# A mixture-of-experts feed-forward over the two chosen experts only, with rows scattered and gathered through memory

## The chip, the cores and the metric

One core of one Trainium2 chip runs the whole kernel: TensorE (PE, with its weight loads shown apart as PEld), VectorE (DVE), ScalarE (ACT), GpSimd (POOL), and SyncE (SP), whose queue here only issues DMAs. The metric is the device time of one execution in microseconds, the median of three runs.

## The reference

Sixty-four sequences of 68 tokens (36 image patches, 32 words), 192 features each, are embedded, pass one quantised attention layer, and then a feed-forward layer with one shared network and eight experts, of which each token uses the best two:

```python
h = h + _L0_attn_ref(_layernorm(h), ...)
h = h + _L0_ffn_ref(_layernorm(h), ...)

def _L0_ffn_ref(x, w_fc_sh, w_proj_sh, w1, w2, router_w, balance_bias):
    shared = _mlp(x, w_fc_sh, w_proj_sh)              # square(relu(x @ wfc)) @ wproj
    scores = jax.nn.sigmoid(xf @ router_w.T)
    _, idx = jax.lax.top_k(scores + balance_bias, 2)
    tw = jnp.take_along_axis(scores, idx, axis=-1)
    tw = tw / (tw.sum(-1, keepdims=True) + 1e-20)
    combine = (jax.nn.one_hot(idx, E) * tw[..., None]).sum(1)
    h = jnp.square(jax.nn.relu(jnp.einsum('nc,ech->neh', xf, w1)))
    y = jnp.einsum('neh,ehc->nec', h, w2)
    return shared + jnp.einsum('nec,ne->nc', y, combine).reshape(x.shape)
```

There are T = 4352 tokens, 34 blocks (TT) of 128, 17 pairs of blocks. All weights are 192 x 192.

## The kernel before

The program is written engine by engine, with semaphores by hand and barriers between stages. The helper `pipeline` (L58) runs stages with lags, unrolls the first steps and loops over the rest. The embedding stage ends in a barrier at 181 us, the attention stages run to 662 us. Their code hardly changes. `split_high` (L668) and `split_low` (L959) split the scaled expert weights in float16 high and low parts, in five chunks laid beside the image steps, and `store_split` (L452) stores them in `w_split` in memory. `load_rest` (L504) loads them and the residual rows `hf` back late in the attention.

**From the projection to the routing.** After `y_scalars` (L1282), ScalarE quantises pairs of blocks (`y_whole`, L794). VectorE adds them (`residual`, L1285) and takes statistics (`stats`, L1292). `deviation` (L1297) follows in two parts. Then, for each pair, VectorE's `normal` (L1306) makes `xf`, ScalarE copies it to float16 (`x2_high`, L803), and VectorE makes the low part (`x2_low`, L1313). TensorE turns the rows (L1606), ScalarE copies them to `XS` (`x2_out`, L808), and `route` (L1594) multiplies them by the router's weights. When all 17 pairs are through, ScalarE takes the sigmoid (L826) and VectorE compares all pairs of experts for all blocks at once (L1336 to L1350, with instructions of 2176 elements). It writes the weight of each expert, zero for six of the eight, as three bfloat16 parts in `C3` (L1352). TensorE turns them to `CT`. A barrier follows.

**The feed-forward.** All nine networks, experts and shared, stand side by side as one of U = 1728 hidden features, in 14 chunks (UC) of 128. `chunks` (L352) walks over 17 groups of 256 tokens and, in each, over the 14 chunks. A chunk goes through `up` (L1628, five matmuls of 256 columns for the float16 parts), `relu` (L836) on ScalarE, `weigh` (L1361) on VectorE, which multiplies by the token's weights that `weights` (L1641) spreads over the partitions by a matmul, `square` (L615) on GpSimd, `high` (L842) on ScalarE, `low` (L1374) on VectorE, and `down` (L1653, six matmuls of 192 columns into one accumulator). The buffers of a chunk are sevenfold (HB). So 17 x (14 x 11 + 8) = 2754 matmuls. `add_h` (L1380) adds the residual, and SyncE stores the group. All matmuls are recorded at L1394, all plain ScalarE copies at L631.

Buffers lie in four big regions (R0, R1, R2, M), which the profile names R or M.

Of the kernel before, what the change touches and what calls it, by code (L numbers as in the profile page):

```python
# [44 lines left out]
HB = 7  # L45
WEIGHED = E * C // P
W2M = UC - 1
# [33 lines left out]
def program(nc, x, x_txt, tok_W, tok_b, tok_pos, embed, W1, b1, W2, b2, w_qkv, b_qkv, w_proj, b_proj,  # L81
            w_fc_sh, w_proj_sh, w1, w2, router_w, balance_bias, ident_c, headmask_c, select_c, lower_c, out):
    ctx = ExitStack()
    with ctx:
# [33 lines left out]
        w_dram = nc.dram_tensor("w_split", [P, 4 * U + 2 * UC * C], F16, kind="Internal").ap()  # L118
# [161 lines left out]
        hf = R2[:, 6144:6144 + TT * C].rearrange("p (i c) -> p i c", i=TT)  # L280

        o16 = [R1[:, 8704 + 512 * k:8704 + 512 * (k + 1)].bitcast(F16).rearrange("p (h t) -> p h t", h=2) for k in range(2)]
        q16 = R2[:, 12672:12672 + 3 * C].bitcast(F16).rearrange("p (a i c) -> p a i c", a=3, i=2)
        xf = R2[:, 13248:13248 + 4 * C].rearrange("p (a i c) -> p a i c", a=2, i=2)
        rows2 = R2[:, 14016:14016 + 4 * C].bitcast(F16).rearrange("p (a i c) -> p a i c", a=2, i=2)
        CT = R1[0:32, 8704:8704 + T // 2].bitcast(BF16)

        hr = R1[:, 0:7 * 256].rearrange("p (a t) -> p a t", a=HB)
        hc = R1[:, 1792:1792 + 7 * 256].rearrange("p (a t) -> p a t", a=HB)
        hs = R1[:, 3584:3584 + 7 * 256].rearrange("p (a t) -> p a t", a=HB)  # L290
        hh = [R1[:, 5376 + 896 * k:5376 + 896 * (k + 1)].bitcast(F16).rearrange("p (a t) -> p a t", a=HB) for k in range(2)]
        ost = R1[:, 7168:7168 + 2 * 2 * C].rearrange("p (a i c) -> p a i c", a=2, i=2)
        sel_b = R1[0:32, 11008:11008 + UC * P // 2].bitcast(BF16)

        w1a = R0[:, 13824:13824 + 2 * U]
        w2a = R1[:, 8456:8456 + UC * C].rearrange("p (m c) -> p m c", m=UC)
        rw_rows = R1[0:E, 11144:11144 + C + C1]
        wst = R0[:, 9216:9216 + 2 * 1344].bitcast(F16).rearrange("p (a k x) -> p a k x", a=2, k=2)
        w2f = w2a.rearrange("p m c -> p (m c)")
        WCH = [(w1a[:, 1152 * k:1152 * (k + 1)], 0, 1152 * k, 2 * U) for k in range(3)]  # L300
        WCH += [(w2f[:, 1344 * k:1344 * (k + 1)], 4 * U, 1344 * k, UC * C) for k in range(2)]
        WCH_AT = [(0, 2), (0, 5), (1, 3), (2, 1), (2, 4)]
        wsplit = R2[:, 0:2 * U + UC * C].bitcast(F16)
        w1s = [R2[:, U * k:U * (k + 1)].bitcast(F16) for k in range(2)]
        w2s = [R2[:, 2 * U + 1344 * k:2 * U + 1344 * (k + 1)].bitcast(F16).rearrange("p (m c) -> p m c", m=UC) for k in range(2)]


        XS = R0[:, T + TT * C:T + TT * C + 3 * T // 2].bitcast(F16).rearrange("p (k t) -> p k t", k=3)
        mv2 = R2[:, 14848:14848 + 2 * TT].rearrange("p (i s) -> p i s", s=2)
        rs2 = R2[:, 14920:14920 + 3 * TT].rearrange("p (k i) -> p k i", k=3)  # L310
        bst2 = R2[:, 15330:15330 + 6 * TT].rearrange("p (i s) -> p i s", i=TT)
# [4 lines left out]
        scr = [R2[:, 15330 + 272 * k:15330 + 272 * (k + 1)].rearrange("p (i e) -> p i e", e=E) for k in range(4)]  # L316

        cmp_a = R0[:, T:T + TT * E * E].rearrange("p (i e f) -> p i e f", e=E, f=E)
        cmp_b = R0[:, T + TT * E * E:T + 2 * TT * E * E].rearrange("p (i e f) -> p i e f", e=E, f=E)
        lower = misc(E * E)  # L320
        sel_w = R0[0:32, 1280:1280 + UC * P]
        xs = R0[:, 0:768].bitcast(F16).rearrange("p (a k t) -> p a k t", a=2, k=3)
        cts = R0[0:32, 1024:1280].bitcast(BF16).rearrange("p (a t) -> p a t", a=2)
        C3 = misc(TT * 16, BF16).rearrange("p (i e) -> p i e", i=TT)
        ex2 = misc(4 * TT).rearrange("p (k i) -> p k i", k=4)
        bmask = misc(4)
        csum = misc(2 * TT).rearrange("p (k i) -> p k i", k=2)


        turns = []  # L330
# [18 lines left out]
        def chunk_rows(m):  # L349
            return P if m < W2M else C1  # L350
# [1363 lines left out]
```

## Time and profile before

| | us |
|---|---|
| median of three runs | 1084.67 (1079.42 to 1090.14) |
| the profiled execution | 1084.4 |
| its span | 1082.6 |
| mean granted clock of TensorE | 0.747 |
| feed-forward stage, in the span | 780.8 to 1079.5 |
| stage from y_scalars to the feed-forward | 694.9 to 780.8 |

Times in the profile are in microseconds from the start of the span unless marked ns. A digit of a slice line is tenths of a fortieth of the span (27.07 us). PEclk is the clock granted to TensorE, in tenths of 2.4 GHz; 0.50 is 1.2 GHz. "Idle before, releaser" tells what ended the engine's idle time ahead of a group.

### The profile page before, as it was taken

The numbers are of one execution on the slowest core, as the hardware profiler recorded it, in microseconds if no ns is written. First come the engines' busy times: TensorE is split into PE (matmuls) and PEld (weight loads), VectorE is DVE, ScalarE is ACT, GpSimd is POOL, SyncE is SP. The second block draws the span as 40 slices with busy tenths as digits, with TensorE's granted clock in tenths as the row PEclk, the third lists the DMA queues.
The fourth block names the chain that finished last, engine by engine and source line by source line (L and its number), as shares of the span: only waits on it lengthen the run. The fifth ranks groups of instructions, "written<-read, shape, count | busy, mean of one in ns | idle before, by whom it ended". The sixth has DMA issues, their size and how long they took to land.

```text
span 1082.6 us, 24294 instructions
## 1 busy us (share of the span) xinstructions
PE 765.0 (71%) x7852; PEld 589.9 (54%) x7852; DVE 806.9 (75%) x1866; ACT 531.8 (49%) x1101; POOL 365.0 (34%) x370
## 2 busy tenths in 40 slices
PE   3699895247724774378888861206399999999998
PEld 2698795146512442145555441105177777777776
DVE  3334551589996999699999979997577777777776
ACT  3123340124427514278888873338155555555554
POOL 2120000358832120132323221000076666666665
PEclk9999798567775555555555555555599999999999
DMA  7942622200002221122222226000000100000000
GB/s 191 250 139 72 175 81 76 84 23 1 0 0 60 74 74 30 38 36 41 39 45 41 43 20 241 9 0 2 16 16 17 32 19 26 23 22 23 22 30 15
DMA packets 114142, 58.11 MB, mean 54 GB/s; under 512 B 75656, under 2 KB 107568, under 8 KB 113968
## 3 DMA queue, kind: packets, MB, share of 16 engines
q1 hardware_dynamic: 112768, 51.24, 18.8%
q0 software_dynamic: 1328, 6.30, 2.0%
q8 instruction: 24, 0.39, 0.1%
q14 instruction: 22, 0.18, 0.1%
HBM read 29.61 MB, written 9.83 MB: 36 GB/s over the span
## 4 chain that ended last, share of the span: by engine, by line
PE 42%; DVE 24%; issue 14%; SPq 9%; DMA 4%; ACT 4%; POOL 3%; DVEq 1%; POOLq 0%; ACTq 0%
PE ps L1394 38%; DMA R<-h_rows 2%; DVE R L1185 2%; DVE M L1091 2%; DVE M L1092 2%; SPq L473 2%; ACT R L631 2%; DVE M L1215 2%; DVE R L1210 1%; PE ps L1468 1%; DVE R L1198 1%; SPq L501 1%; DVE R L1192 1%; SPq L433 1%; DVE R L1290 1%
## 5 line engine op out<-in xcount | busy, mean ns | idle before, releaser
L1394 PE MATMUL ps<-R 128*128 128x192 f16 (+8 forms) x3618 | 460.4, 280 | 32.0 <-DVE R L897 14.4
L1394 PEld LDWEIGHTS ps<-R 128*128 128x128 f16 (+4 forms) x3618 | 348.3, 114 | 120.4 <-issue 59.4
L623 POOL TENSOR_TENSOR R<-R 128x256 f32<-128x256 f32 x238 | 195.5, 828 | 188.3 <-DVE R L1371 186.7
L1371 DVE TENSOR_TENSOR R<-R,ps 64x256 f32<-64x256 f32 (+1 forms) x272 | 114.0, 419 | 62.3 <-ACT R L840 42.4
L1394 PE MATMUL ps<-M 32*128 32x68 bf16 (+2 forms) x1152 | 98.4, 244 | 84.3 <-DMA M<-R 65.9
L840 ACT ACTIVATE R<-ps 128x256 f32<-128x256 f32 x238 | 91.1, 383 | 136.0 <-PE ps L1394 129.0
L631 ACT ACTIVATE R<-ps 68x896 bf16<-68x896 bf16 (+7 forms) x140 | 94.4, 677 | 110.7 <-PE ps L1468 44.9
L1394 PEld LDWEIGHTS ps<-M 32*128 32x128 bf16 (+2 forms) x1152 | 63.1, 115 | 135.3 <-issue 61.1
L631 ACT ACTIVATE R<-R 128x256 f16<-128x256 f32 (+5 forms) x281 | 125.5, 448 | 23.0 <-POOL R L569 20.5
L634 ACT ACTIVATE R<-R,sc 64x512 f16<-64x512 f32 (+12 forms) x106 | 82.8, 838 | 94.0 <-POOL R L586 41.1
L1378 DVE TENSOR_TENSOR R<-R 128x256 f16<-128x256 f32 x238 | 113.0, 476 | 20.1 <-ACT R L631 18.1
L600 POOL TENSOR_TENSOR R<-R,M 128x884 f32<-128x884 f32 x32 | 53.2, 1662 | 146.9 <-ACT M L754 146.9
L1553 PE MATMUL ps<-ident_b,R 128*68 128x128 bf16 x416 | 55.1, 303 | 22.0 <-ACT R L631 20.0
L1394 PE MATMUL ps<-M,R 128*68 128x192 f16 (+2 forms) x430 | 45.0, 258 | 27.1 <-DVE R L1267 26.8
L567 POOL TENSOR_TENSOR R<-R 68x768 f32 (+1 forms) x16 | 23.5, 1467 | 113.3 <-DVEq L1016 108.2
L1480 PE MATMUL ps<-ident,R 68*128 68x68 f32 x64 | 14.3, 295 | 64.2 <-ACT R L631 54.6
L1394 PEld LDWEIGHTS ps<-M,R 128*68 128x68 f16 (+2 forms) x430 | 40.3, 131 | 31.5 <-issue 18.3
L1553 PEld LDWEIGHTS ps<-ident_b,R 128*68 128x68 bf16 x416 | 40.8, 163 | 29.5 <-ACT R L631 26.0
L1394 PE MATMUL ps<-R,M 68*32 68x4 bf16 (+2 forms) x1680 | 54.0, 215 | 2.9 <-DVE R L1030 1.4
L1480 PEld LDWEIGHTS ps<-ident,R 68*128 68x128 f32 x64 | 11.6, 189 | 68.2 <-issue 56.0
L1185 DVE SCALAR_TENSOR_TENSOR R<-ps,sc,M 128x544 f16<-128x544 f32 x64 | 42.6, 707 | 6.9 <-PE ps L1394 5.9
L1394 PEld LDWEIGHTS ps<-R,M 68*32 68x32 bf16 (+1 forms) x1680 | 40.1, 115 | 13.6 <-issue 5.6
(235 smaller groups left out, 1002.0 us busy)
## 6 DMA issues: line engine op xcount, KB each, us to landing
R<-in_x_dram SPq DMA_DIRECT2D x12, 576.0 KB, 8.0
M<-R SPq DMA_DIRECT2D x16, 260.0 KB, 2.3
M<-R SPq DMA_DIRECT2D x32, 130.0 KB, 2.0
R<-h_rows SPq DMA_DIRECT2D x4, 816.0 KB
R<-h_rows SPq DMA_DIRECT2D x1, 3264.0 KB, 14.1
R<-R SPq DMA_DIRECT2D x17, 192.0 KB, 2.5
out_dram<-R SPq DMA_DIRECT2D x17, 192.0 KB, 2.0
R<-w_split SPq DMA_DIRECT2D x1, 3072.0 KB, 20.8
```

Source lines behind the costliest of these rows:

```text
L567: pool.tensor_tensor(v, hb[:, b4, :], mv[:, b4, 0:1].to_broadcast([N, 4, C]), ALU.subtract).then_inc(sem("centred"), 1)
L600: pool.tensor_tensor(L[par], L[par], S[:, par, 1, :].unsqueeze(2).to_broadcast([P, SLOTS, N]), ALU.subtract).then_inc(sem("relative"), 1)
L623: pool.tensor_tensor(hs[0:rows, m % HB, :], hr[0:rows, m % HB, :], other, ALU.mult).then_inc(sem("squared"), 1)
L631: return act.activation(out_, in_, ACT.Copy)
L634: return act.activation(out_, in_, ACT.Identity, scale=scale, bias=bias)
L840: act.activation(hr[0:rows, m % HB, :], ps[0:rows, m % 2, 0:256], ACT.Relu, scale=H_UNIT).then_inc(sem("relu"), 1)
L1185: last = dve.scalar_tensor_tensor(D[:, s0:s0 + 2 * k, :].rearrange("p (a s) k -> p a s k", a=2), score_part(0, part), s1(A_NKK), m.unsquee ...
L1371: last = tt(hc[rows, m % HB, :], hr[rows, m % HB, :], ps[rows, 2 + e % 2, 0:256], ALU.mult)
L1378: tt(hh[1][0:rows, m % HB, :], hs[0:rows, m % HB, :], hh[0][0:rows, m % HB, :], ALU.subtract).then_inc(sem("low"), 1)
L1394: return pe.matmul(o, a, b, start=start, stop=stop, skip_group_check=True)
L1480: pe.transpose(ps[:, 0, k * N:(k + 1) * N], xn[:, par, k, 0:P], ident[0:N, 0:N])
L1553: last = pe.transpose(pPT[:, i, :], slots(Pb[par])[:, at, :], ident_b[:, :])
```

## The change

The shared network still runs over every token, in 17 units of 256 tokens. The experts run only over the rows that chose them. Each expert has a region of CAP = T + 256 rows in a tensor in memory, `x_by_expert`. GpSimd scatters each block's rows there, twice, by the slots of its two experts. The slots are counted on the chip, in three windows of 5, 7 and 5 pairs of blocks. At the end VectorE makes a table, on the chip, of 41 tiles of 256 rows (34 if all were full, and 7 for what is left over): for each its expert and its first row. The pads after each expert's rows are zeroed by DMAs. TensorE and SyncE read the table into registers (`value_load`). Outputs of the tiles go to `y_by_tile` in memory; GpSimd gathers for each block its two rows, and VectorE adds them with their weights to `hf`.

Sixty-eight scatters and 68 gathers are indirect DMAs, of 128 rows of 768 bytes each. Order of the units: 10 shared, 41 routed, 7 shared (58), each with a step on every engine. A step's `down` is three units behind its `up`. Routed tiles are counted ready for the first gathers after 17 tiles, for the second window's after 31, for the third's after 41. `hs`, `hr`, and the hidden PSUM banks are twofold, `hh` and `hl` fourfold.

The diff, cut to its core:

```diff
+TOP = 2
+WB = 2 * 2 * P + 2 * C
+TILE = 256
+ROUTED = TOP * T // TILE + E - 1
+WINDOWS = [(0, 5), (5, 12), (12, 17)]
+SHARED_FIRST = 10
+        SEQ = [("s", i) for i in range(SHARED_FIRST)] + [("r", t) for t in range(ROUTED)] + [("s", i) for i in range(SHARED_FIRST, PAIRN)]
+        LAG = 3
+        READY = [(TOP * P * w.stop + E * (TILE - 1)) // TILE for w in WBLK[:-1]] + [ROUTED]
+        COMBINE_AT = []
+        for i in range(PAIRN):
+            free = SHARED_FIRST + READY[window_of(i)] + LAG + 5
+            COMBINE_AT.append(max(free, COMBINE_AT[-1] + 1.5 if i else 0))
+        COMBINE_AT = [math.ceil(at) for at in COMBINE_AT]
...
+        WCH_AT = [(0, 2), (0, 5), (1, 3), (2, 1), (2, 4), (3, 2)]
+        WCH_DMAS = [4, 8, 4, 2, 2, 2]
...
 @block.sync
-            sp.dma_start(sel_w, select_c).then_inc(sem("ffn_c"), 16)
+            sp.wait_ge(sem("zeros"), 1)
+            for k in range(E - 1):
+                at = E * CAP + TILE * k
+                sp.dma_start(xg[at:at + TILE, :].rearrange("(a p) c -> p a c", p=P), ZT).then_inc(sem("x_zeroed"), 16)
             sp.wait_ge(sem("w_split"), 16)
-            barrier(sp, "sp")
+            sp.wait_ge(sem("table"), 1)
+            for e in range(E):
+                at = sp.value_load(pad_at[0:1, e:e + 1], min_val=0, max_val=(E - 1) * CAP + T)
+                sp.dma_start(xg[bass.ds(at, TILE), :].rearrange("(a p) c -> p a c", p=P), ZT).then_inc(sem("x_zeroed"), 16)
+            sp.wait_ge(sem("x_zeroed"), 16 * (2 * E - 1))
+            sp.wait_ge(sem("scattered"), 16 * TOP * TT)
+            def load_tile(t):
+                wait(sp, "tile_turned", t - 3)
+                at = sp.value_load(table[t:t + 1, 1:2], min_val=0, max_val=XROWS - TILE)
+                sp.dma_start(xr[:, t % 4], xg[bass.ds(at, TILE), :].rearrange("(a p) c -> p a c", p=P)).then_inc(sem(f"xr{t % 4}"), 16)
+            def store_tile(t):
+                sp.wait_ge(sem("y_out"), t + 1)
+                sp.dma_start(yg[TILE * t:TILE * (t + 1), :].rearrange("(a p) c -> p a c", p=P), yr[:, t % 4]).then_inc(sem(f"yr{t % 4}"), 16)
...
 @block.gpsimd
-            chunks([(square, 0)])(pool)
+            pool.memset(ZT, 0.0).then_inc(sem("zeros"), 1)
+            for w, (first, end) in enumerate(WINDOWS):
+                pool.wait_ge(sem("slots"), w + 1)
+                for n in range(2 * first, 2 * end):
+                    for k in range(TOP):
+                        pool.indirect_dma_start(xg, bass.IndirectOffsetOnAxis(ap=slot[:, n, k:k + 1], axis=0), rows2[:, n, :], None).then_inc(sem("scattered"), 16)
+            pool.wait_ge(sem("y_slots"), 1)
+            for i in range(PAIRN):
+                ready = READY[window_of(i)]
+                for a in range(4):
+                    pool.wait_ge(sem(f"yr{a}"), 16 * len(range(a, ready, 4)))
+                wait(pool, "combined", i - 3)
+                for j in range(2):
+                    for k in range(TOP):
+                        pool.indirect_dma_start(gb[:, i % 4, j, k, :], None, yg[0:TILE * ready, :],
+                                                bass.IndirectOffsetOnAxis(ap=y_slot[:, 2 * i + j, k:k + 1], axis=0)).then_inc(sem(f"gathered{i % 4}"), 16)
...
 @block.scalar
+            for i in range(8):
+                y_whole(i)
+            roots(0)
+            y_whole(8)
+            y_whole(9)
+            x2_window(0)
+            sigmoids(0)
...
+            for u in range(UNITS + LAG + 1):
+                t = u - SHARED_FIRST
+                if 1 <= u <= UNITS:
+                    high(u - 1)
+                if 0 <= t + 1 < ROUTED:
+                    x_tile(t + 1)
+                if 0 <= t - LAG - 1 < ROUTED:
+                    y_tile(t - LAG - 1)
+                if u < UNITS:
+                    relu(u)
...
 @block.vector
+            residuals(0, 5)
+            variances(0)
+            residuals(5, 7)
+            deviations(0)
+            normals(0)
+            residuals(7, 9)
+            choose(0)
+            residuals(9, 11)
+            place(0)
+            residuals(11, 12)
+            variances(1)
+            residuals(12, 13)
+            deviations(1)
+            normals(1)
+            residuals(13, 15)
+            choose(1)
+            residuals(15, 17)
+            place(1)
+            variances(2)
+            deviations(2)
+            normals(2)
+            choose(2)
+            place(2)
+            make_table()
+            y_rows()
+            def relu2(u):
+                dve.wait_ge(sem("relu"), u + 1)
+                wait(dve, "low", u - 1)
+                h = ps[:, u % 2, :].rearrange("p (m t) -> p m t", m=2)
+                dve.scalar_tensor_tensor(hs[:, u % 2], h, H_UNIT, hr[:, u % 2], ALU.mult, ALU.mult).then_inc(sem("relu2"), 1)
+            def low(u):
+                dve.wait_ge(sem("high"), u + 1)
+                wait(dve, "h_used", u - 3)
+                tt(hl[:, u % 4], hs[:, u % 2, 0], hh[:, u % 4, 0], ALU.subtract)
+                part = hh[C1:P, u % 4, 1]
+                tt(part, hs[C1:P, u % 2, 1], part, ALU.subtract).then_inc(sem("low"), 1)
...
+            for u in range(STEPS):
+                if 1 <= u <= UNITS:
+                    low(u - 1)
+                if u < UNITS:
+                    relu2(u)
+                if u >= LAG + 1 and u - LAG - 1 < UNITS and SEQ[u - LAG - 1][0] == "s":
+                    add_shared(u - LAG - 1)
+                for i in range(PAIRN):
+                    if COMBINE_AT[i] == u:
+                        combine(i)
...
 @block.tensor
+            def up(u):
+                kind, i = SEQ[u]
+                w = weights_at(u)
...
+                wait(pe, "relu2", u - 1)
+                for m in range(2):
+                    o = ps[:, u % 2, TILE * m:TILE * (m + 1)]
+                    mm(o, w(0, P * m, P), hi, True, False)
+                    mm(o, w(0, P * m, P), lo, False, False)
+                    mm(o, w(1, P * m, P), hi, False, False)
+                    mm(o, w(0, 2 * P + P * m, P), both, False, False)
+                    last = mm(o, w(1, 2 * P + P * m, P), both, False, True)
...
+            for u in range(UNITS + LAG):
+                t = u - SHARED_FIRST
+                if 0 <= t + 1 < ROUTED:
+                    turn_tile(t + 1)
+                if u < UNITS:
+                    load_expert(u)
+                    up(u)
+                if u >= LAG:
+                    down(u - LAG)
```

In words, what is cut out. `turn_tile` turns six blocks of 128 of the loaded tile. `x_tile` copies them (768 elements) out of PSUM to `xs`, `y_tile` copies the 384 output elements of a tile to `yr`. `load_expert` reads the expert's offset into a register, and `weights_at` adds the constant offset of each operand to it. `down` has two times five matmuls of 192 columns. `combine` has four products with sum of 192 elements, with one wait in their middle. `choose` finds the best two of eight by maxima, on 80 or 112 elements; `place` turns counts from two small matmul groups (`rank`) into slots; `make_table` has some 30 instructions on up to 48 elements; `y_rows` has 13 on up to 544. About 22 small VectorE instructions for a triangle of ones and the regions' first rows are added ahead of the first barrier. The weights in `w_split` are laid out by expert, with zero padding gone, 4.1 MB in place of 3.1.

## Rows read from the trace of the kernel before

**Rows 1.** The page: VectorE and the other engines over the span, and TensorE's granted clock.

```profile
PE 765.0 (71%) x7852; PEld 589.9 (54%) x7852; DVE 806.9 (75%) x1866; ACT 531.8 (49%) x1101; POOL 365.0 (34%) x370
...
PEclk9999798567775555555555555555599999999999
```

**Rows 2.** Stages: length, busy PE, PEld, DVE, ACT, POOL, clock, DMA share, GB/s.

```profile
784.00:788.00 4.00, 4.00 (x32) 2.90 (x31) 3.15 (x8) 2.38 (x7) 2.46 (x4) 0.88 0.00 0
...
800.00:1060.00 260.00, 260.00 (x2420) 204.69 (x2418) 196.54 (x463) 143.45 (x418) 171.59 (x209) 1.00 0.08 24
```

**Rows 3.** Groups by form in the feed-forward, 800 to 1060 us.

```profile
L1394 PE MATMUL ps<-R 128*128 128x256 f16 x970 | 137.7, 273 | 0.0
...
L840 ACT ACTIVATE R<-ps 128x256 f32<-128x256 f32 x194 | 74.3, 383 | 109.5 <-PE ps L1394 102.4 <-POOL R L623 7.1
...
L1385 DVE SCALAR_TENSOR_TENSOR R<-ps,sc,R 128x384 f32<-128x384 f32 x15 | 9.3, 618 | 0.5
```

**Rows 4.** Timeline of the routing stage, TensorE: start, length, instructions.

```profile
731.26 0.82 PE L1612 MATMUL ps<-ident_f,R 128*128 128x128 f16 x6 [0.74 <-DVE R L1317]
...
734.05 0.82 PE L1612 MATMUL ps<-ident_f,R 128*128 128x128 f16 x6 [0.48 <-DVE R L1317]
...
751.44 0.72 PE L1394 MATMUL ps<-M,R 128*128 128x8 f16 x20
```

**Rows 5.** Groups by form from 694 to 781 us, ScalarE's copies.

```profile
L631 ACT ACTIVATE R<-ps 128x768 f16<-128x768 f16 x17 | 13.8, 810 | 4.2 <-PE ps L1612 4.1
...
L631 ACT ACTIVATE R<-R 128x384 f16<-128x384 f32 x17 | 8.8, 516 | 2.2 <-DVE R L1310 2.2
```

**Rows 6.** Timeline of the end of the routing, ScalarE and VectorE.

```profile
750.35 0.42 DVE L1317 TENSOR_TENSOR R<-R 128x256 f16<-128x256 f32 x1
...
753.81 0.49 ACT L826 ACTIVATE R<-ps,sc 128x272 f32<-128x272 f32 x1
754.19 1.68 ACT L631 ACTIVATE R<-R 32x1792 bf16<-32x1792 f32 x1
754.33 0.44 DVE L1336 TENSOR_TENSOR R<-R,M 128x272 f32<-128x272 f32 x1 [3.56 <-ACT R L826]
```

**Rows 7.** Groups by form in the attention, 440 to 650 us, VectorE.

```profile
L1210 DVE SCALAR_TENSOR_TENSOR R<-ps,sc,R 128x512 f32<-128x512 f32 x32 | 23.8, 743 | 1.8 <-ACT ps L745 1.8
```

**Rows 8.** Timeline of the attention, SyncE's queue.

```profile
475.26 3.52 SPq L501 DMA_DIRECT2D M<-R  x4
```

**Rows 9.** The page, DMA issues: count, KB each, median us to landing.

```profile
out_dram<-R SPq DMA_DIRECT2D x17, 192.0 KB, 2.0
```

**Rows 10.** Line 98 (waits on a count), TensorE's queue: ns min/median/max, first and last start.

```profile
L98 PEldq FUSED_REGOPS  x65: 37/46/65, 47.6 to 1057.9; - x65
```

**Rows 11.** Timeline of the stage that begins at y_scalars.

```profile
694.87 2.53 ACT L634 ACTIVATE R<-R,sc 128x384 f16<-128x384 f32 x4 [9.99 <-DVEq L1282]
...
699.40 0.30 DVE L1288 TENSOR_SCALAR R<-R,sc 128x384 f16<-128x384 f16 x1
...
700.80 0.30 DVE L1288 TENSOR_SCALAR R<-R,sc 128x384 f16<-128x384 f16 x1
```

**Rows 12.** Timeline of small VectorE instructions in a chain.

```profile
432.63 0.16 DVE L1147 TENSOR_TENSOR sc<-sc 128x1 f32<-128x1 f32 x1
432.83 0.15 DVE L1148 TENSOR_SCALAR sc<-sc 128x1 f32<-128x1 f32 x1
```

**Rows 13.** Timeline behind the first barrier, SyncE's queue.

```profile
181.41 29.10 SPq L473 DMA_DIRECT2D R<-h_rows  x4
```

**Rows 14.** Timeline of GpSimd, two indirect DMAs in a row.

```profile
20.17 0.94 POOL L550 DMA_INDIRECT R<-in_L_txt_tok_embed_dram,R  x1 [9.06 <-PE ps L1419]
21.45 0.94 POOL L550 DMA_INDIRECT R<-in_L_txt_tok_embed_dram,R  x1 [0.34 <-issue]
```

**Rows 15.** Line 550, the sixteen indirect DMAs: ns min/median/max, first and last start.

```profile
L550 POOL DMA_INDIRECT R<-in_L_txt_tok_embed_dram,R x16: 944/945/1103, 8.8 to 87.6; - x16
```

**Rows 16.** Stages again, a stretch of the query, key and value products.

```profile
240.00:260.00 20.00, 15.36 (x108) 12.79 (x107) 17.67 (x27) 8.45 (x17) 16.62 (x12) 0.67 0.00 1
```

More of the change, by code:

```diff
@@ L286, in program @@
[L286 to L293, printed above, removed]
@@ L804, in x2_high @@
                 act.wait_ge(sem("xf"), i + 1)
[L805 to L806 removed]
+                copy(rows2[:, 2 * i:2 * i + 2, 0:C], xf[:, i % 2]).then_inc(sem("x2_high"), 1)
             def x2_out(i):
@@ L848, in _, with sigmoids, x2_window @@
-            chunks([(relu, 0), (high, 3)])(act)
+            def sigmoids(w):
+                t = WBLK[w]
+                act.wait_ge(sem("routed"), WINDOWS[w][1])
+                act.activation(scores[:, t, :], ps[:, 6, t.start * E:t.stop * E].rearrange("p (i e) -> p i e", e=E), ACT.Sigmoid, scale=s1(W_RU)).then_inc(sem("sigmoid"), 1)
+            def x2_window(w):
+                first, end = WINDOWS[w]
+                for i in range(first, end + 1):
+                    if i < end:
+                        x2_high(i)
+                    if i > first:
+                        x2_out(i - 1)
@@ new lines, in _, with x_tile @@
+            for i in range(8):
+                y_whole(i)
+            roots(0)
[3 more added lines that the diff above has]
+            sigmoids(0)
+            for i in range(10, 14):
+                y_whole(i)
+            roots(1)
+            y_whole(14)
+            y_whole(15)
+            x2_window(1)
+            sigmoids(1)
+            y_whole(16)
+            roots(2)
+            x2_window(2)
+            sigmoids(2)
+            def x_tile(t):
+                act.wait_ge(sem("tile_turned"), t + 1)
+                wait(act, "h_psum", SHARED_FIRST + t - 2)
+                copy(xs[:, t % 3], ps[:, 4 + t % 2, :].bitcast(F16)[:, 0:6 * P].rearrange("p (k t) -> p k t", k=3)).then_inc(sem("tile_x"), 1)
@@ L1358, in _ @@
-            barrier(dve, "dve")
-            def weigh(g, m, par, n, half):
-                if m >= WEIGHED:
-                    return
-                first, last_e = m * P // C, (m * P + P - 1) // C
-                dve.wait_ge(sem("relu"), n + 1)
-                dve.wait_ge(sem("c_psum"), g * E + last_e + 1)
-                wait(dve, "squared", n - HB + 1)
-                for e in range(first, last_e + 1):
-                    rows = slice(max(e * C - m * P, 0), min((e + 1) * C - m * P, P))
-                    last = tt(hc[rows, m % HB, :], hr[rows, m % HB, :], ps[rows, 2 + e % 2, 0:256], ALU.mult)
-                last.then_inc(sem("weighted"), 1)
@@ L1388, in _, with residuals, normals @@
-            chunks([(weigh, 0), (low, 3), (add_h, 8)])(dve)
+            def residuals(first, end):
+                for i in range(first, end + 1):
+                    if i < end:
+                        residual(i)
+                    if i > first:
+                        stats(i - 1)
+            def normals(w):
+                first, end = WINDOWS[w]
+                for i in range(first, end + 1):
+                    if i < end:
+                        normal(i)
+                    if i > first:
+                        x2_low(i - 1)
@@ L1604, in route, with turn_rows @@
                 last.then_inc(sem("routed"), 1)
-            for i in range(TT // 2):
+            def turn_rows(i):
                 pe.wait_ge(sem("rows2"), i + 1)
```

549 lines of the change are left out of this document (327 added, 222 removed).

## The prediction

> **What bounds the kernel now.** I read the page's busy line and its slices first: TensorE is busy 71% of the span, but its clock is granted at half from slice 16 to slice 24 and in full over the last quarter [rows 1]. Then the stages. The last one, the feed-forward over all nine networks, runs from 780.8 us to 1079.5 us, 27% of the span. In its middle TensorE is busy in every microsecond (260.00 of 260.00 us, 2420 matmuls, 107.4 ns each), at the full 2.4 GHz, which it reached within 8 us of the stage's start [rows 2]. Some 45% of them are 256 columns wide [rows 3], the rest 192, so 107 and 80 ns at that clock; VectorE and ScalarE have gaps. So this stage is bounded by TensorE's columns. What stands ahead of it from 694.9 us is paced by VectorE. Everything before 694.9 us is nearly untouched.
>
> **Own time.** The profiled execution took 1084.4 us for a span of 1082.6 (1.8 around it); the median is 1084.67. The sum is made in the span, then 1.8 is added.
>
> **TensorE's work.** Before: 17 groups of 162 matmuls, 2754. After: 58 units (17 shared, 41 routed) of 10 matmuls of 256 columns and 10 of 192, and 6 turns of 128 in each routed one: 1160 + 246. At 107.4 ns a unit is 2.15 us; six turns take 0.82 us at half clock [rows 4], some 0.4 at full. So 2.55 us for a routed unit and 2.15 for a shared one: 141 us against 298.7. That 158 us is the most that can be won, if nothing else takes over. Something does.
>
> **The new ring of ScalarE and VectorE.** In a step ScalarE runs high(u-1), x_tile, y_tile, relu(u), in this order; relu2(u) on VectorE needs relu(u), and high(u) needs relu2(u). No part of that overlaps. The rows: ScalarE's 768-element copy out of PSUM 0.81 us and the 384-element one within SBUF 0.52 [rows 5], 256 out of PSUM 0.38 [rows 3]. These give 0.60 for relu (512), 0.49 for y_tile (384), 0.63 for high (512, SBUF), all estimates by length from these rows. One behind another, each starts 0.11 before the end of the one in front (753.81 + 0.49 against 754.19, [rows 6]). VectorE's product from PSUM, 128x512 in float32, stands in the trace: 743 ns [rows 7]. With 0.04 for each change of engine: 0.52 + 0.70 + 0.38 + 0.60 + 0.04 + 0.74 + 0.04 = 3.02 us a routed unit. Before, seven buffers let ScalarE and VectorE run beside each other; the new hs and hr have two. A shared unit has no tile copies; there relu2, add_shared (0.62, [rows 3]) and two subtractions (0.42 each, [rows 6]) give 2.2 us on VectorE.
>
> **What the table costs TensorE's queue.** Weights of a routed unit are addressed by a register that is loaded from the table: one load and 20 matmul operands with it. No row shows either on TensorE. Below: nothing, since 20 small matmuls with constant addresses follow each other every 36 ns [rows 4], so that 26 pairs need 1.0 us of issue, and 2 us of the ring are left. Above: SyncE's DMAs with register addresses come 0.88 us apart (four in 3.52, [rows 8]), 0.13 more than they are busy; 20 x 0.13 = 2.6, plus a load of up to 2.0 (the landing of a store, [rows 9], the nearest thing to a trip to memory), plus 1.0 is 5.6 us a unit. Nearest is the register arithmetic that TensorE's own queue does for its waits, 46 ns a time [rows 10]: 20 x 0.046 + 1.0 for the load + 1.0 = 2.9, just under the ring and not always beside it, so I add 0.2. **A routed unit: 3.2 us (3.0 to 5.6).**
>
> **Walk to the first routed tile.** The start is 694.9 us, ScalarE's first y_whole [rows 11]. Two microseconds are added before it: 22 small VectorE instructions for the triangle and the base rows at about 0.2 [rows 12], between 177.7 us and the barrier that stores held until 181.4 [rows 13], cover most of theirs; the sixth weight chunk and 22 stores in place of 5 lie beside TensorE (bounds 0 to 6).
> VectorE's order until slots(1): 17 pairs of residual and statistics at 1.40 [rows 11], 23.8; the first 0.8; six seams at 0.3, 1.8; twelve pairs of normals at 1.40 (two rounds of turns take 2.79, [rows 4]), 16.8; two starts of that pipeline, 2.5; variances and deviations, 4.9; waits for the sigmoid beyond the residuals that cover it (VectorE stood idle 3.56 us before it, [rows 6]), 1.2; choose(0) and (1), 20 instructions each of 0.16 to 0.44 [rows 6, 12], 11; two places, 3. That is 65.8: slots(1) at 762.7. Window 2 then has no residuals for cover: 21 us to slots(2), 12 more for the table and y_rows (some 45 instructions of 0.2 to 0.5). Shared units start at 795 and would be through ten by 818. Gone from there: the comparisons of 2176 elements, C3, its turns, and two barriers.
> GpSimd: back-to-back indirect DMAs start 1.28 us apart (20.17 and 21.45, [rows 14]). Window 0's 20 scatters are done before slots(1). Window 1's 28 end at 762.7 + 35.8 = 798.5, window 2's 20 queue behind them: 824.1, landed 826. So **the scatters are late, not the shared units.** ScalarE stands at x_tile(0), ahead of relu(9). First load 3 us, turn 0.9, copy 0.8, two units from a half clock: relu2(10) at 836.5.
>
> **To the end.** Window 0's gathers hide. Window 1's 28 wait for routed tile 30, step 44: 836.5 + 34 x 3.2 = 945.3, and 2.5 for the store. From there GpSimd is the bound: 28 + 20 gathers x 1.28 = 61.4: 1009.2. Tile 40 is stored by about 980 (836.5 + 41 x 3.2 + 9.8 for four shared steps with combines + 2.5), before the last 20 begin at 983.6. Combines (four VectorE instructions, 1.6 us each pair) keep up with 5.1 us of gathers, and so do the seven shared units. Last landing 2, combine 1.6, store 2.4 (2.0 of it the landing, [rows 9]): span 1015.2, time **1017**.
>
> **A rule that speaks against it.** The sixteen indirect DMAs of before, issued in the first 88 us, have a median of 945 ns and a minimum of 944 [rows 15], though VectorE is busy 75% of the span [rows 1]. The Trainium skill (SBUF — State Buffer, the "DVE blocks DMA" trap in its section on the doors into it) says that GpSimd can't write descriptors while VectorE runs an instruction in a two-port mode. By that rule the 28 scatters beside the second window's residuals and the third's normals would stretch by an instruction of 0.3 to 0.4 us at each meeting. The rows so far speak against it, so it stands in a rival only.
> TensorE's clock: full over the stage of before; at 0.67 in a stage that is 77% busy with gaps [rows 16]. The Trainium skill (TensorE: Matmul & The Clock Gate, The HAM clock gate) says that half rate is the default and that activity releases it; by that alone the unit, 75% busy, could go either way.
>
> **Rivals.**
> 1. *TensorE's issue takes the bound* and the change is slower. If each unit costs p, GpSimd no longer binds above 3.7 us, and the end is 836.5 + 41 p + 9.8 + 2.5 + 25.6 + 6, so 880.4 + 41 p. It equals the span of before at p = 4.93. At the upper bound, 5.6, the time is 1112. For it: 20 register operands a unit, never seen here on TensorE; against it: 46 ns for its register arithmetic.
> 2. *The clock stays at half* in the routed units. Then 10 x 213 + 10 x 160 + 6 x 107 ns = 4.4 us, time 1063. For it: the 0.67 of [rows 16]. Against it: at 4.4 us TensorE would be busy without a gap, which in the last stage brought the clock up [rows 2].
> 3. *The indirect DMAs are dearer* (contention with VectorE, scatters to memory, which no row shows): 1.7 us in place of 1.28 for 96 on the path adds 40: 1060.
> 4. *It goes better*: ring at 3.0 without queue cost and a shorter walk, 1000 to 1010; below 998 only if gathers or scatters cost under 1.1 us.
>
> **Chances.** Forecast 0.66 (998 to 1042, rival 4's part above 998 in it), rival 1 beyond break-even 0.07, rival 2 0.11, rival 3 0.11, below 998 0.05. The range 998 to 1068 takes in the forecast and most of rivals 2 and 3. Faster by over 1% (a measurement of this kernel can't tell less from no change) 0.89, within 1% 0.04, slower 0.07.
>
> **What the profile after would show.** Right: ScalarE or VectorE idle in turns with a period of 3.0 to 3.6 us in the routed stretch, TensorE busy about three quarters of it at clock 1.00; TensorE idle some 10 us ahead of the first routed tile while GpSimd scatters; indirect DMAs 1.28 apart; and GpSimd in an unbroken row of 48 gathers up to the end. Wrong: TensorE's queue ("issue") as what ended most idle time of the routed units (rival 1), a granted clock of 0.5 there (rival 2), indirect DMAs over 1.5 us apart (rival 3), or shared units after the table that are already through when the first tile lands much later than 829.

## The result, and the profile after

The changed kernel takes **1010.17 us** (median of 4 runs, 1003.54 to 1021.11) against 1083.04 of the kernel before in the same comparison (4 runs): a ratio of 0.9295, 95% interval 0.9243 to 0.9346. The ratio leaves out the slowest of the four executions, more than 1.5% above the fastest. Forecast were 1017.0 us and a range of 998 to 1068. The profiled execution took 1012.82 us for a span of 1010.7.

The page after; the lines of before are in [rows 1].

```profile
PE 616.7 (61%) x6510; PEld 471.8 (47%) x6510; DVE 724.2 (72%) x1723; ACT 480.1 (48%) x826; POOL 304.6 (30%) x269
...
PEclk9799799656797555555555555555555679999995
```

TensorE has 148.3 us less to do (765.0 to 616.7), and only 72 us of it reach the span. From GpSimd's all-reduce that opens the stage (692.9 before, 701.8 now) to the end it is 389.7 us before and 308.9 after: 81 us won, and 9 lost ahead of it. Where the last 309 us go, by stages (length, busy PE, PEld, DVE, ACT, POOL, clock, DMA share, GB/s; [rows 2] is the stage that it replaces):

```profile
702.00:763.00 61.00, 14.90 (x220) 12.84 (x220) 53.19 (x197) 33.90 (x50) 20.13 (x21) 0.50 0.16 53
763.00:829.00 66.00, 26.50 (x242) 20.99 (x242) 45.53 (x152) 18.31 (x31) 47.24 (x49) 0.63 0.29 96
829.00:841.00 12.00, 6.64 (x61) 5.88 (x62) 2.50 (x5) 3.23 (x5) 0.83 (x1) 0.64 0.38 106
841.00:901.00 60.00, 53.35 (x549) 41.68 (x547) 33.97 (x67) 44.57 (x81) 0.18 (x1) 1.00 0.41 121
901.00:943.00 42.00, 36.42 (x366) 27.37 (x365) 28.11 (x62) 31.21 (x57) 19.55 (x20) 1.00 0.71 204
943.00:1004.00 61.00, 31.34 (x288) 24.11 (x285) 39.17 (x90) 20.34 (x39) 46.61 (x48) 0.81 0.51 146
```

No engine binds throughout. VectorE does the walk to the slots, GpSimd the scatters, the units between 841 and 943 us keep TensorE busy for nine tenths at the full clock, and in the last stage TensorE is busy for half and GpSimd for three quarters, with nothing but 0.30 us between two gathers.

GpSimd's timeline (start, length, what; in brackets the idle time ahead of it and what ended it):

```profile
701.77 0.35 POOL L691 PARTITION_ALL_REDUCE sc<-sc  x1 [25.35 <-DVEq L1407]
...
763.15 0.96 POOL L699 DMA_INDIRECT x_by_expert<-R,M  x1 [0.30 <-issue]
768.39 0.96 POOL L699 DMA_INDIRECT x_by_expert<-R,M  x1 [4.28 <-DVEq L1504]
...
828.87 0.96 POOL L699 DMA_INDIRECT x_by_expert<-R,M  x1 [0.30 <-issue]
...
900.82 1.00 POOL L708 DMA_INDIRECT R<-y_by_tile,M  x1 [70.99 <-DMA y_by_tile<-R]
...
925.40 0.94 POOL L708 DMA_INDIRECT R<-y_by_tile,M  x1 [0.30 <-issue]
943.07 0.94 POOL L708 DMA_INDIRECT R<-y_by_tile,M  x1 [16.72 <-DMA y_by_tile<-R]
...
1003.88 0.95 POOL L708 DMA_INDIRECT R<-y_by_tile,M  x1 [0.30 <-issue]
```

Twenty scatters, 4.28 us of waiting for slots(1), then 48 without a stop; 71 us of nothing; twenty gathers, 16.72 us of waiting for tile 30, then 48 without a stop to the end. Most of the 136 start 1.26 us behind the one in front, as in [rows 14]; 1.29 is the mean of either row of 48.

One routed step, in the timeline between two relu2:

```profile
871.92 0.69 DVE L1585 SCALAR_TENSOR_TENSOR R<-ps,R 128x512 f32<-128x512 f32 x1 [0.71 <-ACT R L943]
...
872.65 0.63 ACT L715 ACTIVATE R<-R 128x512 f16<-128x512 f32 x1 [0.76 <-DVE R L1585]
873.18 1.17 ACT L715 ACTIVATE R<-ps 128x768 f16<-128x768 f16 x2
...
874.11 2.17 PE L1628 MATMUL ps<-R 128*128 128x256 f16 x20 [0.35 <-ACT R L715]
874.24 0.60 ACT L943 ACTIVATE R<-ps 128x512 f32<-128x512 f32 x1
...
874.88 0.69 DVE L1585 SCALAR_TENSOR_TENSOR R<-ps,R 128x512 f32<-128x512 f32 x1 [0.71 <-ACT R L943]
```

High, both tile copies, relu, relu2, high: 2.96 us, and each begins where the one in front ends. TensorE waits 0.35 us for ScalarE. The chain that ended last names the same three parts, and its longest pieces stand where they meet (start, length, what):

```profile
828.87 2.32 DMA x_by_expert<-R,M
831.97 2.35 DMA R<-x_by_expert
...
917.78 3.86 DMA R<-x_by_expert
...
1003.88 2.56 DMA R<-y_by_tile,M
```

### The profile page after: what moved, and what is told of

Same layout as the page of the kernel before. It is cut to its first block, busy times and chain, and to the rows that moved or that the text cites. A ratio compares the mean times of both kernels' runs of the same rounds, so it can differ in the third digit from the quotient of the medians.

```text
span 1010.7 us, 20108 instructions
## 1 busy us (share of the span) xinstructions
PE 616.7 (61%) x6510; PEld 471.8 (47%) x6510; DVE 724.2 (72%) x1723; ACT 480.1 (48%) x826; POOL 304.6 (30%) x269
## 4 chain that ended last, share of the span: by engine, by line
DVE 27%; PE 17%; SPq 16%; issue 14%; ACT 10%; POOL 8%; DMA 6%; DVEq 0%; POOLq 0%; ACTq 0%
PE ps L1628 13%; SPq L561 7%; ACT R L715 5%; POOL x_by_expert L699 5%; DVE R L1585 3%; DMA R<-h_rows 3%; SPq L533 2%; DVE M L1221 2%; DVE M L1222 2%; ACT R L943 2%; SPq L540 2%; SPq L541 2%; SPq L539 2%; POOL R L708 2%; PE ps L1702 1%
## 5 line engine op out<-in xcount | busy, mean ns | idle before, releaser
L1628 PE MATMUL ps<-R 128*128 128x256 f16 (+6 forms) x2024 | 297.9, 302 | 59.9 <-DVE R L1585 13.1
L1628 PEld LDWEIGHTS ps<-R 128*128 128x128 f16 (+3 forms) x2024 | 215.0, 129 | 116.0 <-issue 63.6
L715 ACT ACTIVATE R<-ps 128x768 f16<-128x768 f16 (+5 forms) x217 | 139.0, 658 | 112.6 <-PE ps L1702 43.7
L1628 PE MATMUL ps<-M 32*128 32x68 bf16 (+4 forms) x1192 | 101.9, 246 | 101.0 <-DMA M<-R 68.0
L1628 PEld LDWEIGHTS ps<-M 32*128 32x128 bf16 (+3 forms) x1192 | 65.8, 116 | 153.4 <-issue 61.4
L718 ACT ACTIVATE R<-R,sc 128x512 f16<-128x512 f32 (+11 forms) x107 | 83.8, 839 | 97.2 <-POOL R L666 41.0
L715 ACT ACTIVATE R<-R 128x512 f16<-128x512 f32 (+4 forms) x101 | 64.7, 642 | 90.3 <-DVE R L1585 63.2
L708 POOL DMA_INDIRECT R<-y_by_tile,M x68 | 67.2, 988 | 107.8 <-DMA y_by_tile<-R 88.0
L699 POOL DMA_INDIRECT x_by_expert<-R,M x68 | 67.4, 991 | 59.6 <-DVEq L1504 39.5
L1585 DVE SCALAR_TENSOR_TENSOR R<-ps,R 128x512 f32<-128x512 f32 x58 | 40.1, 692 | 41.8 <-ACT R L943 41.0
```

What stands on the lines that cost most here:

```text
L699: pool.indirect_dma_start(xg, bass.IndirectOffsetOnAxis(ap=slot[:, n, k:k + 1], axis=0), rows2[:, n, :], None).then_inc(sem("scattered"), 16)
L708: pool.indirect_dma_start(gb[:, i % 4, j, k, :], None, yg[0:TILE * ready, :], bass.IndirectOffsetOnAxis(ap=y_slot[:, 2 * i + j, k:k + 1], ...
L715: return act.activation(out_, in_, ACT.Copy)
L718: return act.activation(out_, in_, ACT.Identity, scale=scale, bias=bias)
L1585: dve.scalar_tensor_tensor(hs[:, u % 2], h, H_UNIT, hr[:, u % 2], ALU.mult, ALU.mult).then_inc(sem("relu2"), 1)
L1628: return pe.matmul(o, a, b, start=start, stop=stop, skip_group_check=True)
```

## The experiments

All times within the stage are counted below from GpSimd's all-reduce that opens it (701.77 above). In three profiled executions of the changed kernel that start itself lay at 701.8, 695.1 and 710.0 us, a spread wider than what most of the edits below can change. What follows it agrees within 0.7 us: last gather at +302.1, +301.6 and +301.4, end at +308.9, +308.4 and +308.2.

**1. On a first chip: addresses, ScalarE's order, fourteen shared units first.** Four kernels on one chip.

```diff
 e1_static_weights
-expert_at.append(pe.value_load(table[i:i + 1, 0:1], min_val=0, max_val=E * WB))
+expert_at.append(WB * (i % E))
 e2_relu_first
+if u < UNITS: relu(u)
 if 0 <= t + 1 < ROUTED: x_tile(t + 1)
 if 0 <= t - LAG - 1 < ROUTED: y_tile(t - LAG - 1)
-if u < UNITS: relu(u)
 e3_fourteen_first
-SHARED_FIRST = 10
+SHARED_FIRST = 14
```

The first leaves out the table's choice of the expert: each tile is computed with expert t mod 8. The fourth kernel is the one of before.

> Weights of the routed tiles at constant addresses (expert t mod 8 in place of the table's), so TensorE's queue loads no register; the routed outputs are those of other experts. My theory (the ring of ScalarE and VectorE sets the routed step): step 2.95 us as in the changed kernel, time within 3 us of it. The rival (TensorE's queue, about 1.0 us of register work a unit): step 2.5 to 2.6 us, 10 to 14 us faster, and the idle time ahead of up that ended by 'issue' or by x_tile gone.

> ScalarE runs relu(u) ahead of the two tile copies, so these lie beside relu2 of VectorE. My theory: the ring shrinks by the part of 1.17 us of copies that relu2 (0.69) now covers; step 2.95 to some 2.5 us, where TensorE (2.5 us of work) is next; the last gathers start 34 x 0.4 = 12 to 15 us earlier and, as 48 gathers behind them take 61 us whatever the step, the time falls by the same 12 to 15 us. The rival (TensorE or its queue already bounds the step): no change.

> Fourteen shared units ahead of the routed ones in place of ten. My theory: TensorE's idle 16 us in front of the first tile shrinks to some 7 us, but the scatters and the 48 gathers are where they were: time within 3 us of the changed kernel. The rival (that idle time is what is lost): 8 to 9 us faster.

> The kernel before, again, for its stages. In the changed kernel the all-reduce ahead of y_scalars ends 8.9 us later than before: 2 at the first barrier, 4 to 5 in the loads and statistics behind it, 3 in the attention loop. If these 7 us are the spread from run to run, this profile shows some of it (all-reduce before y_scalars anywhere from 689 to 700 us); if they are the change's, it is at 692.9 within 1 us.

Measured: 1086.31, 1085.69 and 1093.35 us, ratios to before 0.9998 (0.9956 to 1.004), 1.0004 (0.9958 to 1.005) and 1.012 (1.0064 to 1.0176); before again took 1080.03. Three different edits, and each seemed to cost the whole gain. Their traces show one and the same pattern. From the waits of the relu-first kernel, 740 to 870 us (engine, line, waited for: us in total, times, longest):

```profile
POOL x_by_expert L699 <- DVEq L1504: 68.9, 3, 35.2
ACT R L715 <- remote: 42.2, 4, 17.8
```

ScalarE stands still four times, up to 17.8 us, on nothing that another engine does. That pushes slots(1), whose wait is 4.28 us above, to 19.8:

```profile
764.30 0.96 POOL L699 DMA_INDIRECT x_by_expert<-R,M  x1 [0.30 <-issue]
785.06 0.95 POOL L699 DMA_INDIRECT x_by_expert<-R,M  x1 [19.80 <-DVEq L1504]
```

The times of this chip say nothing of the three edits. Either each of them moved something that opens holes, or the holes belong to the chip. But between the holes the routed units run undisturbed, and there the traces do speak. With constant addresses the unit is what it is in the changed kernel, as the theory put down for this run had it: 2.95 us over 18 steps from +185 to +238; two relu2 of that stretch:

```profile
912.15 0.69 DVE L1585 SCALAR_TENSOR_TENSOR R<-ps,R 128x512 f32<-128x512 f32 x1 [0.70 <-ACT R L943]
915.11 0.69 DVE L1585 SCALAR_TENSOR_TENSOR R<-ps,R 128x512 f32<-128x512 f32 x1 [0.71 <-ACT R L943]
```

So the registers cost the changed kernel's unit nothing, and the ring of ScalarE and VectorE holds it. With relu first most steps there are 2.73 to 2.76 us. What fourteen shared units do to the time stays open: that kernel was run on this chip alone.

**2. The changed kernel again, on another chip.**

> The changed kernel, unaltered, as a control of its variants. Theory A (the 75 us that the three variants were over the changed kernel belong to the chip or to the placement of the tensors, not to the edits): this one comes to 1075 to 1095 us too, with holes of 10 us and more in the row of scatters around 755 to 790 us and PE waiting for nothing the profile shows. Theory B (each edit moved code or work so that the holes opened): this one stays at 1003 to 1021 us with scatters in an unbroken row.

1006.53 us (1005.23 to 1015.43), ratio 0.928 (0.922 to 0.934), an unbroken row of scatters. Theory B as it was worded, but the chip was another one, so it settles nothing between the two.

**3. Four beside each other: unaltered, relu first, other windows, both.** The second is the same file as on the first chip.

```diff
 e8_windows_7_6_4
-WINDOWS = [(0, 5), (5, 12), (12, 17)]
+WINDOWS = [(0, 7), (7, 13), (13, 17)]
```

The residuals, y_whole and roots that are written out between the windows move with them, by one or two pairs.

> The changed kernel once more, as the mark for the three runs beside it on this chip. Theory A (holes belong to the chip): on a chip with holes 1075 to 1095 us, on one without 1003 to 1015. Theory B (holes belong to the altered code): 1003 to 1021 here whatever its neighbours show.

> ScalarE's relu(u) ahead of x_tile and y_tile, the same edit as before, now with the unedited kernel beside it. Theory A: it stands within 2% of the unedited one; if the routed unit is bound by the ring (high, x_tile, y_tile, relu, relu2 in a row, 2.955 us), the unit falls to ScalarE's own sum, 2.5 to 2.6 us, and window 1's gathers and the end come 8 to 13 us sooner. Theory B: 60 to 80 us slower than the unedited one. If TensorE's queue bound the unit (registers), nothing moves: within 3 us.

> Windows of 7, 6 and 4 pairs in place of 5, 7 and 5. If the first routed tile waits for the scatters behind slots(1), 40 instead of 48 of them stand ahead of it: it comes about 9 us sooner. If the end is bound by GpSimd's gathers, 40 instead of 48 follow window 1's last tile, which comes two units (5.9 us) later: the end another 4 us sooner. Together 10 to 14 us faster than the unedited one. If instead VectorE's walk or TensorE's units bind, within 3 us of it.

> Both edits together. If ring, scatters and gathers are three separate terms of the sum, the gains add: 20 to 27 us faster than the unedited kernel, 980 to 990 us on a chip without holes.

Measured in this order: 1012.07 (ratio 0.9337, 0.9284 to 0.939), 1012.87 (0.9345, 0.9282 to 0.9407), 1009.35 (0.9319, 0.9265 to 0.9374) and 1012.45 (0.9351, 0.9295 to 0.9407). The relu-first file takes 1085.69 us on the first chip and 1012.87 here, so **the 73 us are not the edit's**: they belong to that chip, or to something else that held while it was used, such as the placement of the tensors, which was not tried apart. "remote" stands nowhere among the waits of these traces. The edits themselves do next to nothing. Gains of 8 to 13, 10 to 14 and 20 to 27 us had been expected of the three, and all three expectations missed; the reasons can be read.

*Relu first* did shorten the unit, from 2.95 to 2.79 us (mean of 14 steps from +145 to +184). In its timeline TensorE's 20 matmuls and 6 turns now follow each other at 2.74, and ScalarE waits for them:

```profile
875.18 2.27 PE L1628 MATMUL ps<-R 128*128 128x256 f16 x20 [0.17 <-DVE R L1585]
...
876.49 0.60 ACT L943 ACTIVATE R<-ps 128x512 f32<-128x512 f32 x1 [0.55 <-PE ps L1628]
```

But window 0's gathers began at +199.6, as before (+199.1 to +199.9), and window 1's at +241.8 (before +241.2). The order puts y_tile behind relu, so each output is stored a little later in its step. And once the gathers run, TensorE waits for the loads of some tiles. From its waits, 901 to 945 us:

```profile
PEld ps L1883 <- DMA R<-x_by_expert: 3.1, 4, 1.4
```

The unaltered kernel on the same chip has nearly the same wait over the same stretch (2.8 us, longest 1.6), and its steps stay at 2.95 there: the ring covers it. With relu first TensorE has no such slack, and steps of up to 4.1 us occur beside the gathers. So the 0.2 us a unit are given back before the tile that the 48 gathers wait for.

*Windows of 7, 6 and 4* missed because the theory looked at one wait alone. The row of 68 scatters then starts with slots(0), later, and never stops:

```profile
743.20 1.20 POOL L699 DMA_INDIRECT x_by_expert<-R,M  x1 [41.98 <-DVEq L1502]
...
829.98 0.96 POOL L699 DMA_INDIRECT x_by_expert<-R,M  x1 [0.30 <-issue]
914.18 1.00 POOL L708 DMA_INDIRECT R<-y_by_tile,M  x1 [83.24 <-DMA y_by_tile<-R]
...
1000.49 0.94 POOL L708 DMA_INDIRECT R<-y_by_tile,M  x1 [0.30 <-issue]
```

+43.0 to +129.8, against +36.3 to +127.1: the only slack there ever was is the 4.28 us ahead of slots(1), and the first window's later start eats it. The gathers are the same case: they begin at +214.0, after tile 20, and run through; of the gap of 15.8 us in the kernel beside it, 14.2 are paid at the start. So with this cut GpSimd's two rows of 68 (87 to 88 us each) bind, and a cut can only shift GpSimd's idle time. The last gather came at +300.3, 1.1 us sooner than in the kernel beside it. With both edits it came at +300.9.

**4. A cut between the two, half the gathers, and constant addresses.** Three on a further chip.

```diff
 e10_windows_6_6_5
-WINDOWS = [(0, 5), (5, 12), (12, 17)]
+WINDOWS = [(0, 6), (6, 12), (12, 17)]
 high(u - 1)
-x_tile(t + 1)
 y_tile(t - LAG - 1)
 relu(u)
+x_tile(t + 1)
 e11_half_gathers
-for k in range(TOP):
+for k in range(1):
     pool.indirect_dma_start(gb[:, i % 4, j, k, :], None, yg[0:TILE * ready, :], ...
 e12_static_6_6_5 = e10_windows_6_6_5, and
-expert_at.append(pe.value_load(table[i:i + 1, 0:1], min_val=0, max_val=E * WB))
+expert_at.append(WB * (i % E))
```

The second leaves the second expert's outputs ungathered, the third the choice of the expert.

> Windows of 6, 6 and 5 pairs, and ScalarE's step in the order high, y_tile, relu, x_tile. Times from the all-reduce that opens the stage (the changed kernel: first gather +199 to +200, window 1's gathers +241.3, last gather +302, span +308 to +309). If GpSimd's row of gathers sets the end and its idle 16 us between windows 0 and 1 is what can be won: unit 2.74 us, first gather at +201, no gap or one under 4 us before window 1's, last gather at +287 to +291, so 10 to 15 us faster than the changed kernel, about 0.92 of before. If the faster unit is given back to late tile loads beside the gathers, as in the relu-first run: 3 to 6 us faster.

> The changed kernel with the second expert's gathers left out (34 in place of 68). If 48 gathers in a row set the end: window 1's begin at +241 as before, 14 end at +259, the last window's 10 wait for tile 40's store at about +268 and end by +282: about 20 us faster than the changed kernel. If the routed units or the shared units behind them set the end all the same: within 3 us.

> The first kernel of this call with constant weight addresses in place of the registers (expert t mod 8; the table's choice of the expert is left out). If register work in TensorE's queue holds the unit at 2.74 us once the ring no longer does: 2.5 to 2.6 us a unit, ScalarE's own sum. If the columns and the waits hold it: 2.7 and over, and less than 2 us of change in the time.

*Windows 6, 6, 5 with the new order*: **1003.52 us** (6 runs, 999.64 to 1007.44), ratio 0.9237 (0.9196 to 0.9278). The lowest of all that compute the whole layer; against the changed kernel's own ratios (0.928 to 0.9337) it is half a per cent to one, on different chips, and its interval overlaps those of two of the three. The trace is plainer: last gather at +295.1, end at +301.9, both 6.2 to 7.1 us sooner. That is less than the 10 to 15 of the first theory and a little more than the 3 to 6 of the second. The unit was 2.87 us where 2.74 was expected, and of the gap before window 1 6.17 us are left:

```profile
901.84 0.99 POOL L708 DMA_INDIRECT R<-y_by_tile,M  x1 [75.74 <-DMA y_by_tile<-R]
...
938.54 1.03 POOL L708 DMA_INDIRECT R<-y_by_tile,M  x1 [6.17 <-issue]
```

The two edits were not run apart, but the row can be counted. This cut leaves 44 gathers behind tile 30 in place of 48, worth 5 us at 1.29 each, and they begin at +239.7 in place of +241.2 to +241.3. So about 5 of the 6.5 us are the cut's, won out of the gap, and only 1.5 come from earlier tiles.

*Half the gathers*: 993.26 us, ratio 0.916 (0.9108 to 0.9211); last gather at +285.5, end at +295.2, 13 us sooner, where about 20 were expected. So the gathers do set the end, but the next bound lies only 13 us behind. It is seen in GpSimd's waits from 890 us on:

```profile
POOL R L708 <- DMA y_by_tile<-R: 96.0, 4, 71.6
POOL R L708 <- DVE R L1607: 22.2, 7, 5.4
```

GpSimd now waits for VectorE's combines (L1607) to free the four buffers, and these stand in VectorE's order among the last routed and the shared units. Those end where they did: last relu2 at +275.4, in the changed kernel at +275.2.

*Constant addresses*: 997.14 us, ratio 0.9173 (0.9119 to 0.9227), an interval that overlaps that of its pair; in the traces the end is at +295.4, 6.5 us sooner than its pair's. The unit is 2.66 us in place of 2.87 (means over 18 steps), between the two expectations. One step of it, relu2 to relu2:

```profile
875.78 0.69 DVE L1583 SCALAR_TENSOR_TENSOR R<-ps,R 128x512 f32<-128x512 f32 x1 [0.41 <-ACT R L942]
878.44 0.69 DVE L1583 SCALAR_TENSOR_TENSOR R<-ps,R 128x512 f32<-128x512 f32 x1 [0.41 <-ACT R L942]
```

So the registers in TensorE's queue cost about 0.2 us a unit, once ScalarE and VectorE no longer hide them. In the kernel as changed they are hidden, as the 2.95 us of experiment 1 show: there the ring holds the unit.

## Why the prediction was right

The sum, term by term, in microseconds of span:

| term | forecast | measured |
|---|---|---|
| start of the stage (all-reduce) | 694.9 | 701.8 |
| to window 1's first scatter | 67.8 | 66.6 |
| 48 scatters | 61.4 | 61.4 |
| to relu2(10) | 12.4 | 10.7 |
| to window 1's first gather | 111.3 | 102.5 |
| 48 gathers | 61.4 | 61.8 |
| landing, combine, store | 6.0 | 5.9 |
| end | 1015.2 | 1010.7 |

The bounds and the order of the waits came as forecast. That the sum is within 4.5 us of the span is in part luck: a start 6.9 us later than forecast stands against 8.8 us too many for the routed units and 2.9 for the walk and the first tile.

- **TensorE's columns as the most to be won, and other bounds in their place**: right. 148.3 us gone from TensorE, 72 from the span.
- **The start, 2 us (0 to 6)**: mis-sized; this is the term that failed. It measured 8.9 us between the two profiled executions, outside its bounds. Of these, 2.0 lie ahead of the loads behind the first barrier, which SyncE issues at 183.44 instead of 181.41 ([rows 13]). The triangle makes 1.2 of them: from the end of TensorE's matmuls to this issue it is 5.5 us in place of 4.2. TensorE itself ends 0.8 later. The other 6.9 lie behind, 1.4 in the row of issues and 4.3 in the landing of the last load. That load in three executions, the changed kernel's profiled one, its repeat of experiment 2, and the one of before:

```profile
204.45 28.28 DMA R<-h_rows
202.38 24.13 DMA R<-h_rows
200.98 23.99 DMA R<-h_rows
```

  The forecast had put the 22 weight stores beside TensorE and had not asked what they do to the loads that follow. But they do not explain the 28.3. All twelve profiled executions of the changed kernel and its variants have these stores, and all edits lie behind this place. In nine of them the load takes 22.9 to 24.5 us, in three 28.3 to 29.2; in the two of before 24.0 and 23.4. From the issue of the loads to the all-reduce it is 510.7 to 513.7 us in the nine, 518.3 to 519.6 in the three, and 511.5 and 508.6 before. So most of the 6.9 is spread between executions of the same code, for which the bounds of 0 to 6 left no room. Ahead of the loads the changed code does come later: they are issued at 182.4 to 191.9 us in the twelve, 186.7 in the mean, against 181.4 and 178.8 before. Of these 6.5 us the triangle is 1.2; what makes the rest was not tried, and two executions of before are few. In all, the all-reduce stands at 700.5 us in the mean of the twelve and at 692.9 and 687.4 in the two of before, about 10 us where the forecast had 2.
- **The walk of VectorE, 65.8 us from the first y_whole**: right within 1.2 us, although no row showed the sum. Its nine terms were not measured one by one, so errors in them may cancel.
- **48 scatters in a row behind slots(1), at 1.28**: right, 61.4 us, and TensorE idle for 16.0 us ahead of the first turn, until the tile's load landed (forecast some 10).
- **To relu2(10), 12.4**: 10.7, the landing and the load being quicker together by 1.7.
- **The unit, 3.02 from the ring and 0.2 for TensorE's queue**: the mechanism was right, the size not. The ring measures 2.955 (0.60, 0.69, 0.63 and 1.17 for both copies, against 0.60, 0.74, 0.63 and 0.81 + 0.49 with 0.11 of overlap), and the 0.2 on top was not there: 8.8 us too many over the 34 steps. Constant addresses show why: in the changed kernel's order they leave the unit at 2.95, and only in the new order, where the ring no longer covers it, does the register work show, with 0.2 us.
- **The price of the registers**: the load takes 306 ns in TensorE's queue against 1.0 us assumed, with 151 ns of arithmetic behind it; each further piece costs 46 ns as in [rows 10], but some 12 of them a unit, not 20. Line 1900 and line 1628 in TensorE's queue (ns least/median/most, first and last start):

```profile
L1900 PEldq TENSOR_LOAD <-M x41: 297/306/528, 836.7 to 952.8; - x41
L1900 PEldq FUSED_REGOPS  x41: 151/151/165, 837.3 to 953.2; - x41
...
L1628 PEldq FUSED_REGOPS  x492: 42/46/46, 837.7 to 962.4; - x164
```

  That is 0.306 + 0.151 + 12 x 0.046 = 1.0 us a unit in place of 1.9. Rival 1 (a unit of 4.93 us and more) is out by far.
- **48 gathers in a row to the end**: right, and halving them took 13 us off the end.
- **Rival 2, the clock**: out. It is 1.00 from 841 to 943 us, in which TensorE is busy for nine tenths (forecast three quarters). The Trainium skill (TensorE: Matmul & The Clock Gate, The HAM clock gate) lets activity release it; the trace agrees, and the 0.81 of the last stage, half busy, costs nothing there, since the gathers set its end.
- **Rival 3, dearer indirect DMAs**: out, since it wanted 1.7 us each. Line 699 has a median of 960 ns, and the 48 on the path took what was forecast, with VectorE busy for 46 of the 66 us. The rule quoted from the Trainium skill (SBUF — State Buffer, the "DVE blocks DMA" trap) is not refuted by that, only its price is small here. Seven of the 48 took 1.03 to 1.22 us, and of the 20 ahead of them five in a row, beside VectorE's normals of the second window, took 1.07 to 1.12, while the pairs of normals between them took 0.85 in place of 0.67 (748 to 755 us). Which mode these instructions ran in no trace here shows.
- **Readings of the prediction that do not hold**, none of which enters the sum. The clock stands at half from slice 13 to slice 29 of [rows 1], not from 16 to 24. Columns alone do not fill the last stage of before: the matmuls of 256 columns, 48% of them in the trace, at 107 ns and the others at 80 would take 93 ns in the mean, against 107.4 measured; the sum used the 107.4, and 20 matmuls of a unit took 2.15 to 2.17 us, as forecast. Rival 3's sum gives 1057, not 1060.

The range's other end deserves a word. On one chip, three variants of the changed kernel took 1086 to 1093 us, over the range and no faster than before. The unaltered changed kernel was not run on that chip.

## What to carry to other kernels

Once work is moved to rows chosen at run time, count the indirect DMAs before the arithmetic: 136 of them at 1.29 us are 175 us of GpSimd, more than the 158 us of TensorE that the change saves at most, and only what of them lies beside other work is free. Where two rows of one queue each have a small gap, re-cutting the windows can win that gap and no more; it pays to sum the queue's own work from its first release before moving a cut. And run the unedited kernel beside its variants, on the same chip: without it three edits looked like losses of 75 us, of which the one that was run again elsewhere cost nothing.

## What was not expected of the hardware

**Holes in which an engine waits for no other, on one chip alone.** The relu-first file is identical in both traces. From 738 to 766 us, with 20 scatters in each, the packets of the DMA queues (queue, kind: packets, MB, share) are these on the chip with holes:

```profile
q0 software_dynamic: 928, 1.94, 20.1%
```

and on the one without:

```profile
q0 software_dynamic: 960, 1.97, 20.5%
q8 instruction: 1, 0.02, 0.3%
q14 instruction: 2, 0.02, 0.2%
```

On the first chip the three instruction packets come at 770 to 775 us, when the scatters have stopped (last start 764.30). ScalarE goes on at 768.18 after 12.93 us; which engine's code a packet brings the trace does not say. The same again at the end of the scatters: last start 858.33, ScalarE on at 862.47 after 11.73 us, TensorE until then with single matmuls 1.4 to 2.1 us apart.

```profile
858.33 0.96 POOL L699 DMA_INDIRECT x_by_expert<-R,M  x1 [0.30 <-issue]
...
862.41 0.48 PE L1628 MATMUL ps<-R 128*128 128x192 f16 x2 [1.78 <-issue]
...
862.47 0.60 ACT L943 ACTIVATE R<-ps 128x512 f32<-128x512 f32 x1 [11.73 <-remote]
```

That would fit engines that run straight-line code faster than it is brought in, because the code's packets wait behind dense indirect DMAs; it is not shown. And it is not strict, since one packet of either queue passed at 799 to 801 us amid scatters, and ScalarE went on before the first of the three was seen. The kernel of before, with 16 indirect DMAs, at most two in a row, took its usual time on that chip (1080.03 us, and 1083.01 in the median of 19 more). Why this chip shows it and the three of the later experiments do not stays open; so does the cause, since no run there changed the code's length or the density of the scatters.

**What was not tried.** SyncE's wait for all 68 scatters could be shortened, since the first tiles hold rows of the first windows alone. But they are loaded from one tensor at an address from the table, while scatters to addresses from the slots are still under way in it; nothing in the program orders the two, so it was left as it is.
